# Two graph attention layers on one core: later loads moved into the timetable, two buffers for x2, and new orders of the first and last turns

## The chip, the cores and the metric

The kernel runs on one core of a Trainium2 chip. The time is device microseconds of one execution, the median of several runs. The core's engines are TensorE (PE, matrix products and transposes), VectorE (DVE), ScalarE (ACT), GpSimd (POOL) and SyncE (SP, which here only issues DMA transfers). Each works through its own instructions in their written order; between engines there are only semaphores.

## The reference

128 graphs of 128 nodes with 256 features go through two layers. Shortened:

```python
# layer A: attention, four hops, norm
q, k, v = (x @ W.T + b for W, b in ...)              # 8 heads of 32
p = softmax(where(adj == 0, -16384, q @ k.T))
z = v
for _ in range(4):
    z = 0.9 * (p @ z) + 0.1 * v
x = norm(x + z) * gamma + beta
# layer B: attention with an edge bias, then an MLP
n = norm(x) * ln1_g + ln1_b
p = softmax(q @ k.T / sqrt(32) + where(adj > 0, 0.1 * adj * adj, -inf))   # q, k, v of n
x = x + (p @ v) @ wo + bo
n = norm(x) * ln2_g + ln2_b
out = x + gelu(n @ w1 + b1) @ w2 + b2
```

## The kernel before

The 128 graphs are taken as 64 pairs. All work on a pair is cut into 84 named steps, such as `qA` (the q projection of layer A) or `z0` (the first hop), and the step of pair g is written `qA.g`. One list, the timetable, puts all steps of all pairs in an order. Every engine walks the whole list and does its own part of each step, waiting on semaphores; so the list fixes the order of instructions on each engine and nothing else. There is no other planner.

The middle of the list is made from `ORDER`: in a turn each step is done once, with a lag that says for which pair. The first 9 turns are replaced by the written-out list `HEAD`, the last 8 by `TAIL`, in which pairs are counted from the end (`d1.1` is of the last pair, `d1.2` of the one before it). 52 turns stay between.

The names, with the engine in brackets where it is not PE and an evacuation:
- `lt`, `lx`, `laA`, `laB`, `st` [SP]: load x transposed, x, the adjacency of layer A and of B; store the output. `xs` [POOL] splits x transposed into a high and a low part.
- `qA kA vA`, `qB kB vB`: projections, each of 12 products of 256 columns; q and k are evacuated by ACT, v by DVE. `sA`, `sB`: scores.
- `msA`, `msB` [POOL] masks, `eb` [DVE] the edge term for `msB`. `mA00` to `mA11` [DVE] add the mask and take row maxima, `eA00` to `eA11` [ACT] the exps, `rA0`, `rA1` [DVE] reciprocals, `wA0`, `wA1` [POOL] normalise in two halves each, `pA00` to `pA11` turn the probabilities (evacuated by ACT or DVE). The first digit is the graph of the pair. The same with B.
- `z0` to `z3`: hops, evacuated by ACT; `h0` to `h3`: turned back, evacuated by DVE. `xv` [POOL]: the share of v plus x.
- `y0 i0 n0`, `y1 i1 n1`, `y2 i2 n2`: norms, as statistics [DVE], root [POOL], scaling [DVE]. `g`, `b1`, `b2` [POOL]: gamma and beta, plus bo, plus b2. `tB`, `tC`: turn the normed rows, split by ACT (high) and DVE (low).
- `pv`: probabilities times v, split by ACT and DVE. `o`: output projection; DVE adds it into the tile `x2`. `u0` to `u3`: first MLP product with gelu on ACT (four instructions each), `c0` to `c3` [DVE] its low part; `d0`, `d1`: second MLP product, 24 products each, added into `x2` by DVE and stored.
- Once only: `Wf`, the fold of the norms' biases into the projections' biases, PE with products of one column; `Wq Wk Wv Wo Wu0 Wu1 Wd0` to `Wd3`, the splits of weights into high and low (high on ACT, low on DVE, for `Wd` on POOL).

PE's results go to a ring of 4 PSUM banks in list order (`table.bank`); a step waits until the one four before it is evacuated. The scores have banks of their own.

Ahead of its part of the list SP issues, in this order: Wq of A, x transposed of pair 0, Wk and Wv of A, adjacency A of pair 0, wq wk wv of B, w1 with two columns, x of pair 0, wo, w2 in four parts, three columns, five rows (each spread over 128 partitions). ACT issues four columns and one row of its own. The raw weights lie in tiles that the pairs use later: wq, wk, wv, wo in `probs`, w1 in `probsT_B`, w2 in `x1b`, `nx`, `n2`, `x2`. DVE's `output` (L752) waits until both halves of `x2` of the pair before are stored.

Of the kernel before, what the change touches and what calls it, by code (L numbers as in the profile page):

```python
# [55 lines left out]
wA1.2 n1.0 z2.1 xv.2 b1.0 i0.1 wA0.2 qA.3 laA.1 h2.1 tB.0 g.1 z3.1 pA10.2 pA11.2 h3.1 rA0.2 y0.1 n0.1 mB00.0 kB.0 xs.4
lt.3 mB01.0 qB.0 kA.3 sB.0 mB10.0 pA00.2 pA01.2 mB11.0 eB00.0 y1.1 vA.3 i1.1 eB10.0 rB1.0 lx.1 eB11.0 vB.0 z0.2 n1.1
eB01.0 laA.2 wB1.0 rB0.0 sA.3 kA.4 h0.2 pB10.0 mA00.3 tB.1 pB11.0 z1.2 pB00.0 mA01.3 pB01.0 eA00.3 h1.2 eA01.3 kB.1
mA10.3 rA0.3 mA11.3 wB0.0 xv.3 pv.0 laA.3 eb.1 wA0.3 z2.2 qB.1 h2.2 msB.1 eA10.3 o.0 pA00.3 y2.0 eA11.3 mB00.1 mB01.1
rA1.3 sB.1 i2.0 laB.1 mB10.1 b1.1 n2.0 z3.2 wA1.3 msA.4 mB11.1 eB00.1 qA.4 vA.4 h3.2 eB10.1 tC.0 eB01.1 laA.4 pA01.3  # L60
mA00.4 rB0.1 sA.4 pA10.3 eB11.1 pA11.3 xv.4 mA01.4 wB0.1 u0.0 vB.1 eb.2 y0.2 c0.0 rB1.1 z0.3 u1.0 i0.2 lt.4 pB00.1
h0.3 lx.2 u2.0 n0.2 c1.0 u3.0 wB1.1 c2.0 pB01.1 c3.0 z1.3 pB10.1 pB11.1 y1.2 mA10.4 n1.2 mA11.4 eA00.4 g.2 b2.0 eA10.4
h1.3 lx.3 d0.0 eA01.4 pv.1 rA0.4 d1.0 eA11.4 tB.2 rA1.4 qA.5 o.1 y2.1 i1.2 kB.2 qB.2 pA00.4 z2.3 sB.2 pA10.4 n2.1
eB00.2 mB00.2 xs.5 h2.3 mB01.2 msB.2 mB10.2 mB11.2 kA.5 lt.5 tC.1 msA.5 z3.3 wA0.4 vB.2 eB10.2 lx.4 eB01.2 h3.3 pA01.4
laB.2 y0.3 vA.5 eB11.2 u0.1 b1.2 laA.5 i2.1 rB0.2 u1.1 rB1.2 n0.3 pA11.4 c0.1 wA1.4 eb.3 u2.1 u3.1 c1.1 c2.1 y1.3 c3.1
mA00.5 lx.5 sA.5 z0.4 pB00.2 pB01.2 n1.3 pB10.2 mA01.5 eA00.5 i0.3 eA01.5 wB0.2 mA10.5 st.0 h0.4 lt.6 rA0.5 d0.1 tB.3
g.3 wB1.2 d1.1 eA10.5 laA.6 z1.4 mA11.5 i1.3 pB11.2 kB.3 h1.4 qB.3 z2.4 pv.2 eA11.5 sB.3 eB00.3 mB00.3 h2.4 rA1.5
mB01.3 pA00.5 o.2 y2.2 mB10.3 z3.4 mB11.3 qA.6 n2.2 eB01.3 h3.4 b2.1 y0.4 pA10.5 vA.6 rB0.3 kA.6 tC.2 vB.3 n0.4 eB10.3
pA01.5 eB11.3 msB.3 pA11.5 u0.2 u1.2 wA0.5 xs.6 xv.5 rB1.3 wA1.5 i2.2 b1.3 msA.6 mA00.6 b2.2 laB.3 lt.7 c0.2 sA.6 i0.4
y1.4 c1.2 z0.5 mA01.6 u2.2 wB0.3 u3.2 mA10.6 g.4 n1.4 qA.7 h0.5 pB10.3 eb.4 xs.7 st.1 tB.4 i1.4 wB1.3 c2.2 pB00.3  # L70
msB.4 mA11.6 z1.5 pB01.3 qB.4 laB.4 eA00.6 pB11.3 kB.4 eA01.6 c3.2 pv.3 xv.6 laB.5 h1.5 rA0.6 wA1.6 eA10.6 lx.6 eA11.6
d0.2 d1.2 wA0.6 rA1.6 mB00.4 mB01.4 sB.4 z2.5 mB10.4 o.3 eB00.4 eB01.4 eB10.4 y2.3 h2.5 rB0.4 i2.3 vA.7 wB0.4 kA.7
n2.3 b2.3 pA00.6 pA10.6 z3.5 mB11.4 pA01.6 tC.3 sA.7 eB11.4 pA11.6 h3.5 y0.5 rB1.4 pB00.4 n0.5 u0.3 st.2 z0.6 u1.3
c0.3 mA00.7 u2.3 mA01.7 c1.3 h0.6 u3.3 c2.3 msA.7 y1.5 c3.3 pB10.4 vB.4 eA00.7 mA10.7 laA.7 b1.4 z1.6 n1.5 pB01.4 d0.3
eA01.7 tB.5 eA10.7 pB11.4 mA11.7 eb.5 rA1.7 eA11.7 d1.3 h1.6 i0.5 qB.5 rA0.7 lt.8 kB.5 pv.4 mB00.5 z2.6 sB.5 pA00.7
# [5 lines left out]
laA.4 lt.3 h3.6 xs.4 wA0.5 tC.8 y0.6 eB10.7 z0.5 wA1.5 vA.4 eB11.7 eb.6 vB.7 h0.5 u0.8 sA.4 mA00.4 n0.6 z1.5 pB00.7  # L81
xv.5 c0.8 u1.8 i2.8 lx.5 h1.5 msA.4 u2.8 u3.8 rB1.7 qA.3 z2.5 c1.8 c2.8 b1.7 mA01.4 pB10.7 xs.3 c3.8 y1.6 pB01.7
pB11.7 eA00.4 n1.6 h2.5 laB.5 d0.8 eA01.4 pv.7 mA10.4 rA0.4 wB0.7 z3.5 mA11.4 tB.6 i0.6 d1.8 rA1.4 b2.8 eA10.4 h3.5
y0.5 g.6 eA11.4 wB1.7 o.7 y2.7 qB.6 kB.6 msB.6 pA10.4 pA00.4 pA01.4 pA11.4 eB00.6 mB00.6 sB.6 n2.7 z0.4 n0.5 kA.3
mB01.6 mB10.6 tC.7 eB01.6 i1.6 h0.4 mB11.6 wA0.4 eB10.6 xv.4 vB.6 rB0.6 eb.5 y1.5 vA.3 mA00.3 n1.5 eB11.6 c0.7 lx.4
st.8 c1.7 u0.7 sA.3 z1.4 u1.7 rB1.6 pB00.6 u2.7 wA1.4 h1.4 tB.5 mA01.3 u3.7 mA10.3 z2.4 laA.3 msA.3 pB01.6 pB10.6
pB11.6 eA00.3 qB.5 h2.4 kB.5 c2.7 z3.4 c3.7 mA11.3 mB00.5 eA01.3 rA0.3 eA10.3 pv.6 mB01.5 eA11.3 sB.5 rA1.3 d0.7
eB10.5 mB10.5 i2.7 lx.3 i0.5 d1.7 eB00.5 h3.4 y0.4 pA10.3 mB11.5 o.6 y2.6 vA.2 b1.6 eB01.5 g.5 qA.2 eB11.5 rB0.5 kA.2
n0.4 n2.6 lt.2 pA11.3 pA00.3 vB.5 wB0.6 pA01.3 rB1.5 tC.6 y1.4 mA00.2 mA01.2 sA.2 z0.3 u0.6 n1.4 h0.3 qA.1 u1.6 mA10.2
c0.6 i1.5 laA.2 pB00.5 eb.4 c1.6 tB.4 u2.6 u3.6 xv.3 pB01.5 qB.4 wB1.6 c2.6 b2.7 eA10.2 msB.5 kB.4 eA00.2 xs.2 c3.6  # L90
pB10.5 lt.1 lx.2 pB11.5 mA11.2 mB00.4 eA11.2 d0.6 rA1.2 sB.4 wA0.3 z1.3 mB01.4 pv.5 d1.6 msA.2 eA01.2 h1.3 eB00.4
rA0.2 eB01.4 mB10.4 pA10.2 laB.4 mB11.4 o.5 wA1.3 y2.5 z2.3 pA00.2 st.7 pA11.2 pA01.2 h2.3 i0.4 kA.1 z0.2 n2.5 z3.3
tC.5 h0.2 eB10.4 rB0.4 eB11.4 vB.4 i2.6 h3.3 y0.3 b1.5 mA00.1 g.4 u0.5 xs.1 i1.4 sA.1 z1.2 rB1.4 n0.3 pB00.4 u1.5 c0.5
pB01.4 h1.2 wB0.5 b2.6 laB.3 u2.5 c1.5 pB10.4 mA01.1 u3.5 pB11.4 c2.5 wB1.5 c3.5 z2.2 mA10.1 laA.1 pv.4 eA00.1 y1.3
h2.2 eb.3 st.6 eA01.1 st.5 n1.3 eA10.1 d0.5 msB.4 rA0.1 wA1.2 d1.5 msA.1 wA0.2 mA11.1 tB.3 z3.2 i2.5 o.4 b1.4 eA11.1
y2.4 rA1.1 wB0.4 h3.2 n2.4 qB.3 kB.3 y0.2 i0.3 wB1.4 mB00.3 g.3 mB01.3 pA00.1 sB.3 tC.4 xv.2 n0.2 pA10.1 eB00.3 mB10.3
mB11.3 pA11.1 vA.1 eB01.3 pA01.1 i1.3 eB10.3 eB11.3 b2.5 rB0.3 y1.2 vB.3 rB1.3 u0.4 z0.1 c0.4 n1.2 u1.4 pB00.3 wA0.1
pB01.3 msB.3 u2.4 c1.4 i2.4 wA1.1 h0.1 tB.2 i0.2 u3.4 pB10.3 b1.3 g.2 wB0.3 eb.2 i1.2 pB11.3 c2.4 kB.2 c3.4 qB.2 wB1.3
xv.1 pv.3 z1.1 mB00.2 mB01.2 sB.2 mB10.2 d0.4 mB11.2 lx.1 d1.4 eB00.2 rB0.2 msB.2 h1.1 o.3 eB01.2 y2.3 eB10.2 z2.1
b2.4 eB11.2 h2.1 n2.3 pB00.2 z3.1 rB1.2 pB01.2 h3.1 laB.2 tC.3 y0.1 vB.2 pB10.2 n0.1 u0.3 c0.3 wB0.2 i2.3 u1.3 pB11.2  # L100
# [830 lines left out]
```

## Time and profile before

| what | us |
|---|---|
| runs | 2314.32, 2314.19, 2317.76 |
| median | 2314.32 |
| the profiled execution | 2317.23 |
| its span | 2315.4 |
| PE busy | 2266.6 (98%) |
| ACT busy | 1926.8 (83%) |
| DVE busy | 1749.9 (76%) |
| POOL busy | 1520.4 (66%) |

The span goes from the first to the last instruction of the core; the execution's own time has 1.8 us around it. Busy times count instructions at work. Products are pipelined, so their durations overlap and the distance from start to start is what counts. The granted clock is TensorE's, as a share of 2.4 GHz; half of it is the other level, 1.2 GHz.

### The profile page before, as it was taken

What the parts mean: (1) busy time and instruction counts of PE and PEld (TensorE: products, weight loads), DVE (VectorE), ACT (ScalarE), POOL (GpSimd) and SP (SyncE); (2) the same over time, 40 slices, a digit from 0 to 9 for tenths busy, and PEclk for the clock granted to TensorE, in tenths of its full rate; (3) what the DMA queues carried; (4) which work ended last, traced back from release to release, by engine and by line L of the source; (5) the groups of instructions that cost most, each with busy time, mean ns of one, the idle gap of its engine ahead of it and who ended that gap; (6) DMA issues with size and microseconds to landing.
All of it is one profiled execution on the core that took longest, in us unless ns stands there. A gap on an engine that the chain in (4) does not pass through costs nothing. (4 is left out here: it accounts for less than half of the span.)

```text
span 2315.4 us, 78263 instructions
## 1 busy us (share of the span) xinstructions
PE 2266.6 (98%) x29492; PEld 2154.3 (93%) x29492; DVE 1749.9 (76%) x6993; ACT 1926.8 (83%) x6478; POOL 1520.4 (66%) x1613
## 2 busy tenths in 40 slices
...
DMA packets 95781, 76.88 MB, mean 33 GB/s; under 512 B 9648, under 2 KB 95152, under 8 KB 95408
## 3 DMA queue, kind: packets, MB, share of 16 engines
q1 hardware_dynamic: 94176, 71.73, 10.0%
...
q10 hardware_dynamic: 1232, 0.14, 0.0%
...
## 5 line engine op out<-in xcount | busy, mean ns | idle before, releaser
L580 ACT ACTIVATE probs<-probs,negmax 128x128 f32<-128x128 f32 x2048 | 797.0, 398 | 28.1 <-DVE negmax L704 22.0
L862 POOL TENSOR_TENSOR probs<-probs,rinv 128x512 f32<-128x512 f32 x512 | 534.3, 1064 | 138.7 <-DVE rinv L718 138.4
L580 ACT ACTIVATION_READ_ACCUMULATOR probs<-probs,negmax 128x1 f32 x2048 | 402.3, 196 | 0.0
L601 ACT ACTIVATE zT<-ring_ps 128x512 f32<-128x512 f32 x256 | 157.8, 617 | 182.4 <-PE ring_ps L459 182.2
L377 PE MATMUL ring_ps<-inT_C_high,w_high 128*128 128x256 f32 x1024 | 302.4, 295 | 5.3 <-DVE inT_C_low L675 4.0
L515 PE MATMUL ring_ps<-w_high,hT_high 128*128 128x256 f32 x1024 | 296.8, 290 | 1.0 <-DVE hT_low L790 1.0
L451 PE MATMUL ring_ps<-ident,probs 128*128 128x128 f32 x2048 | 293.3, 276 | 3.1 <-ACT hT_high L621 1.6
L515 PE MATMUL ring_ps<-w_low,hT_high 128*128 128x256 f32 x1024 | 286.5, 280 | 0.0
L515 PE MATMUL ring_ps<-w_high,hT_low 128*128 128x256 f32 x1024 | 286.2, 279 | 0.0
L377 PE MATMUL ring_ps<-inT_C_high,w_low 128*128 128x256 f32 x1024 | 285.8, 279 | 0.0
L377 PE MATMUL ring_ps<-inT_C_low,w_high 128*128 128x256 f32 x1024 | 285.8, 279 | 0.0
L790 DVE TENSOR_TENSOR hT_low<-hidden,hT_high 128x512 fp32r<-128x512 f32 x256 | 231.4, 905 | 62.5 <-ACT hT_high L621 56.2
L451 PEld LDWEIGHTS ring_ps<-ident,probs 128*128 128x128 f32 x2048 | 227.4, 141 | 29.5 <-issue 26.9
L704 DVE CUSTOM_DVE_ANT_0 probs<-score_ps,mask_B 128x128 f32<-128x128 f32 x1024 | 228.4, 283 | 29.2 <-PE score_ps L442 29.2
L868 POOL TENSOR_TENSOR rstd<-moments,eps 128x2 f32<-128x2 f32 x192 | 39.4, 205 | 313.3 <-DVE moments L773 312.9
L704 DVE CUSTOM_DVE_ANT_0 probs<-score_ps,mask_A 128x128 f32<-128x128 f32 x1024 | 229.5, 283 | 4.3 <-PE score_ps L442 3.1
L621 ACT ACTIVATE hidden<-ring_ps,b_col 128x256 f32<-128x256 f32 x512 | 218.8, 490 | 13.9 <-PE ring_ps L377 9.9
L621 ACT ACTIVATE hT_high<-ring_ps,b_col 128x256 fp32r<-128x256 f32 x512 | 220.9, 503 | 0.0
L459 PE MATMUL ring_ps<-probsT_A,z 128*32 128x128 f32 x6144 | 209.2, 277 | 1.2 <-DVE z L738 1.0
L757 DVE TENSOR_TENSOR x<-ring_ps,x1b 128x512 f32<-128x512 f32 x64 | 44.2, 690 | 209.9 <-PE ring_ps L377 203.6
L377 PEld LDWEIGHTS ring_ps<-inT_C_high,w_high 128*128 128x128 f32 x1024 | 194.7, 190 | 7.9 <-DVE inT_C_low L675 4.8
L377 PEld LDWEIGHTS ring_ps<-inT_C_low,w_high 128*128 128x128 f32 x1024 | 195.2, 191 | 0.0
...
## 6 DMA issues: line engine op xcount, KB each, us to landing
xT_sb<-in_xT_dram SPq DMA_DIRECT2D x64, 256.0 KB, 3.1
x_sb<-in_x_dram SPq DMA_DIRECT2D x64, 256.0 KB, 2.8
out_dram<-x SPq DMA_DIRECT2D x128, 128.0 KB, 1.9
...
qT_B<-in_L_gnn_Wq_dram SPq DMA_DIRECT2D x1, 256.0 KB, 3.6
kT_B<-in_L_gnn_Wk_dram SPq DMA_DIRECT2D x1, 256.0 KB, 4.8
```

Source lines behind the costliest of these rows:

```text
L377: mm = pe.matmul(dst, left(a, kc), right(b, kc), start=(n == 0), stop=(n == len(pairs) - 1))
L451: mm = pe.transpose(ring(name, g)[:, r * P:(r + 1) * P], probs[:, UNIT[l, b], half * HR + r, :], ident[:, :])
L459: mm = pe.matmul(ring(name, g)[r * HD:(r + 1) * HD, (b * C + c) * P:(b * C + c + 1) * P], src[:, b, h * HD:(h + 1) * HD], prT[:, b, h, :], ...
L515: mm = pe.matmul(ring(name, g)[:, 0:H], hT[a][:, f, b * P:(b + 1) * P], w2_p[c][:, f, :], start=(n == 0), stop=(n == len(pairs) - 1))
L580: e = act.activation(probs[:, u, h, :], probs[:, u, h, :], ACT.Exp, bias=negmax[:, u, h:h + 1], scale=-1.0, accum_out=sums[:, u, h:h + 1])
L601: act.activation(zT[k][:, :, :, :], ring(name, g).rearrange("p (b c n) -> p b c n", b=GB, c=C), ACT.Copy).then_inc(s_out[name], 1)
L621: e = act.activation(dst[:, i, :], ring(name, g)[:, i * T:(i + 1) * T], ACT.Gelu, bias=b1_col[:, 2 * f + i:2 * f + i + 1])
L704: t = dve.tensor_tensor_reduce(probs[:, u, h, :], score_ps[:, r, (b * C + half) * P:(b * C + half + 1) * P], mask[l][:, b, :], -1.0, HIGHE ...
L757: dve.tensor_tensor(x2[:, :, :], ring(name, g).rearrange("p (b n) -> p b n", b=GB), x1b[:, :, :], ALU.add).then_inc(s_out[name], 1)
L790: dve.tensor_tensor(hT[1][:, 2 * f:2 * f + 2, :], hidden[:, f % 2, :, :], hT[0][:, 2 * f:2 * f + 2, :], ALU.subtract).then_inc(s_h_low, 1)
L862: pool.tensor_tensor(probs[:, u, hs, :], probs[:, u, hs, :], rinv[:, u, hs].unsqueeze(2).to_broadcast([P, HR, P]), ALU.mult).then_inc(s_pr ...
L868: pool.tensor_tensor(rstd[n][:, :, :], moments[n][:, :, 1:2], eps[:, :].unsqueeze(1).to_broadcast([P, GB, 1]), ALU.add).then_inc(s_shifted ...
```

## The change

- SP issues ahead of the list only x transposed of pair 0 and the three weights of layer A. All other loads become steps: `LB` (wq, wk, wv), `Lc` (three columns and the row bvB), `Lu` (w1 and two columns), `Lo` (wo), `Ld` (w2), `Lr` (four rows); the first `laA` and `lx` now issue too. SP's list begins laA.0 LB.0 laB.0 Lc.0 lt.0 Lu.0 laA.1 lx.0 lt.1 laB.1 Lo.0 Ld.0 lt.2 laA.2 lx.1 Lr.0. The semaphore `rest` is parted into `columns` (waited for by `fold`) and `rows` (by `scale_shift`).
- `x2` has two buffers, used by even and odd pairs, each with its semaphore; `output` of pair g waits for the store of pair g - 2. The same index stands in `store`, `spread`, `norm`, `down` and `plus_b2`.
- `HEAD` and `TAIL` are new orders of the same steps. PE's part of the new head begins qA.0 kA.0 vA.0 sA.0 Wf.0 vA.1 qA.1 kA.1 pA10.0 pA11.0 pA00.0 pA01.0 sA.1 z0.0 h0.0 z1.0 kA.2 h1.0 qA.2 z2.0, and ACT's Wk.0 Wq.0 qA.0 kA.0 Wu1.0 eA00.0 eA10.0 eA11.0 eA01.0 Wu0.0 qA.1 Wv.0 kA.1 pA10.0 pA00.0 Wd2.0 z0.0. `ORDER` stays.

Of the two lists, the beginning of the first and the end of the second are shown.

```diff
-eb.0 qA.0 lx.0 laB.0 xs.0 laA.0 kA.0 eA00.0 vA.0 mA00.0 sA.0 msA.0 eA01.0 xs.1 mA01.0 lt.0 qA.1 lt.1 mA10.0 mA11.0
...
+laA.0 xs.0 Wk.0 Wq.0 LB.0 eb.0 laB.0 mA00.0 qA.0 mA01.0 msA.0 mA10.0 kA.0 Lc.0 Wu1.0 mA11.0 eA00.0 vA.0 lt.0 xs.1 sA.0
+Wf.0 rA1.0 msB.0 eA10.0 wA1.0 vA.1 wA0.0 Lu.0 eA11.0 rA0.0 msA.1 eA01.0 Wu0.0 qA.1 Wv.0 kA.1 pA10.0 pA11.0 pA00.0
+laA.1 xv.0 pA01.0 sA.1 Wd2.0 eb.1 xs.2 mA00.1 z0.0 mA01.1 eA00.1 eA01.1 mA10.1 h0.0 xv.1 eA10.1 mA11.1 wA0.1 rA0.1
+wA1.1 z1.0 msA.2 Wd1.0 eA11.1 kA.2 h1.0 qA.2 z2.0 lx.0 rA1.1 pA00.1 Wd0.0 Wd3.0 h2.0 pA01.1 pA10.1 pA11.1 mA00.2 z3.0
...
-u1.2 u2.2 c0.2 c1.2 c2.2 c3.2 u3.2 i2.2 pB10.1 pB00.1 b2.2 pB11.1 b1.1 pB01.1 wB0.1 d0.2 pv.1 d1.2 o.1 y2.1 wB1.1 n2.1
-tC.1 i2.1 c0.1 u0.1 u1.1 c1.1 u2.1 u3.1 c2.1 c3.1 d0.1 d1.1 st.1 b2.1
+u0.3 wB1.2 pB10.2 qB.1 rB0.2 kB.1 wB0.2 pB00.2 pB01.2 c0.3 msB.1 u1.3 i2.2 wB0.1 pB11.2 u2.3 c1.3 b1.1 pv.2 u3.3 c2.3
+mB00.1 sB.1 c3.3 eB00.1 o.2 eB01.1 y2.2 mB01.1 st.2 mB10.1 n2.2 eB10.1 d0.3 rB0.1 mB11.1 d1.3 tC.2 vB.1 eB11.1 rB1.1
+pB00.1 pB01.1 c0.2 u0.2 pB10.1 u1.2 pB11.1 u2.2 c1.2 pv.1 c2.2 c3.2 u3.2 o.1 y2.1 n2.1 d0.2 tC.1 d1.2 c0.1 u0.1 c1.1
+u1.1 u2.1 wB1.1 u3.1 c2.1 c3.1 i2.1 d0.1 b2.2 b2.1 st.1 d1.1
...
+SET_UP = {"LB": ("load_proj",), "Lu": ("load_up",), "Lo": ("load_wo",), "Ld": ("load_down",), "Lc": ("load_columns",),
+          "Lr": ("load_rows",), "Wf": ("fold",), "Wo": ("split_o",)}
...
-        x2 = sb("x2", [P, GB, H])
+        x2 = [sb(f"x2_{i}", [P, GB, H]) for i in range(2)]
...
-        w2_raw = [x1b, nx, n2, x2]
+        w2_raw = [x1b, nx, n2, x2[0]]
...
-            weight(rawA["q"][:, :, :], WqT, "Aq")
             sp.dma_start(xT_sb[:, :, :], xT_v[0]).then_inc(s_xT, 16)
-            weight(rawA["k"][:, :, :], WkT, "Ak")
-            weight(rawA["v"][:, :, :], WvT, "Av")
-            sp.dma_start(adj_sb["A"][:, :, :], adj_v[0]).then_inc(s_adj["A"], 16)
...
+            for n, w in (("q", WqT), ("k", WkT), ("v", WvT)):
+                weight(rawA[n][:, :, :], w, "A" + n)
+
+            def load_proj(name, g):
+                for n, w in (("q", wq), ("k", wk), ("v", wv)):
+                    weight(rawB[n], w, "B")
+
+            def load_up(name, g):
+                weight(w1_raw, w1, "up")
+                column(h2_col, ln2_b, "up")
+                column(g2_col, ln2_g, "up")
+
+            def load_wo(name, g):
+                weight(rawB["o"], wo, "o")
+
+            def load_down(name, g):
+                for f, t in enumerate(w2_raw):
+                    sp.dma_start(t[:, :, :], w2.rearrange("(c p) n -> p c n", p=P)[:, 2 * f:2 * f + 2, :])\
+                        .then_inc(s_in["down"], 16)
+
+            def load_columns(name, g):
+                for t, w in ((colB["q"], lbq), (colB["k"], lbk), (b1_col, b1)):
+                    column(t, w, "columns")
+                row(bvB_row, lbv, "columns")
+
+            def load_rows(name, g):
+                for t, w in ((gamma_row, gamma), (beta_row, beta), (bo_row, bo), (b2_row, b2)):
+                    row(t, w, "rows")
...
-                if g or l == "B":
-                    sp.dma_start(adj_sb[l][:, :, :], adj_v[g]).then_inc(s_adj[l], 16)
+                sp.dma_start(adj_sb[l][:, :, :], adj_v[g]).then_inc(s_adj[l], 16)
...
-                    sp.dma_start(out_v[g][:, b, :], x2[:, b, :]).then_inc(s_stored, 16)
+                    sp.dma_start(out_v[g][:, b, :], x2[g % 2][:, b, :]).then_inc(s_stored[g % 2], 16)
...
-                if g:
-                    dve.wait_ge(s_stored, 16 * GB * g)
-                dve.tensor_tensor(x2[:, :, :], ring(name, g).rearrange("p (b n) -> p b n", b=GB), x1b[:, :, :],
+                if g >= 2:
+                    dve.wait_ge(s_stored[g % 2], 16 * GB * (g // 2))
+                dve.tensor_tensor(x2[g % 2][:, :, :], ring(name, g).rearrange("p (b n) -> p b n", b=GB), x1b[:, :, :],
```

## Rows read from the trace of the kernel before

**Rows 1.** Windows: length, busy us of each engine, granted clock, DMA share, GB/s.
```profile
16.00:28.00 12.00, 0.17 (x1) 0.17 (x2) 2.93 (x21) 1.03 (x5) 2.11 (x3) 0.68 0.49 126
28.00:60.00 32.00, 27.58 (x369) 23.78 (x370) 18.39 (x75) 24.82 (x89) 23.54 (x22) 0.85 0.14 43
60.00:76.00 16.00, 16.00 (x118) 14.69 (x119) 12.22 (x47) 9.51 (x37) 11.21 (x13) 0.68 0.15 43
76.00:320.00 244.00, 240.66 (x3208) 225.55 (x3207) 195.10 (x762) 204.83 (x695) 164.81 (x174) 1.00 0.10 31
320.00:1980.00 1660.00, 1660.00 (x21869) 1585.89 (x21867) 1276.00 (x5197) 1427.85 (x4814) 1124.17 (x1190) 1.00 0.10 32
1980.00:2264.00 284.00, 277.45 (x3569) 261.98 (x3571) 221.51 (x825) 230.56 (x766) 180.84 (x191) 1.00 0.09 28
2264.00:2291.00 27.00, 21.06 (x204) 19.75 (x204) 14.26 (x54) 16.61 (x54) 7.47 (x8) 0.87 0.02 6
2291.00:2316.00 25.00, 15.46 (x102) 14.54 (x100) 6.73 (x14) 6.72 (x17) 2.16 (x3) 0.80 0.05 17
```

**Rows 2.** Timeline of SP's queue, 4 to 29 us: start, us, line, transfer.
```profile
4.49 0.77 SPq L308 DMA_DIRECT2D probs<-in_L_gnn_wv_dram  x1
...
14.97 2.67 SPq L314 DMA_DIRECT2D bvB_row<-in_L_gnn_bv_dram  x1
...
19.58 0.43 SPq L344 DMA_DIRECT2D adj_B<-in_adj_dram  x1
20.05 8.11 SPq L338 DMA_DIRECT2D xT_sb<-in_xT_dram  x2
```

**Rows 3.** Timeline of all engines, first 43 us; in brackets the idle time before.
```profile
13.12 0.84 ACT L572 ACTIVATE kT_A<-ring_ps,colA_k 128x256 f32<-128x256 f32 x2 [1.72 <-PE ring_ps L377]
...
25.07 0.42 DVE L670 SCALAR_TENSOR_TENSOR edges<-adj_B 128x256 f32<-128x256 int32 x1 [15.69 <-DMA adj_B<-in_adj_dram]
...
27.83 0.58 PE L377 MATMUL ring_ps<-inT_A_high,wA_q_high 128*128 128x256 f32 x1 [11.97 <-POOL inT_A_low L843]
...
42.15 1.08 PE L459 MATMUL ring_ps<-probsT_A,v_A 128*32 128x128 f32 x32
```

**Rows 4.** Sources L388 and L391, the fold: ns min/median/max, first and last start.
```profile
L388 PE MATMUL ring_ps<-h_col,probsT_B x32: 250/352/353, 63.5 to 69.0; 128*128 128x1 f32 x32
...
L388 PE MATMUL ring_ps<-h_col,probs x16: 169/250/251, 61.8 to 63.4; 128*128 128x1 f32 x16
...
L391 PE MATMUL ring_ps<-probs,h_col x4: 634/634/774, 69.2 to 70.6; 128*128 128x256 f32 x4
```

**Rows 5.** Timeline, the last 53 us.
```profile
2263.85 1.17 PE L442 MATMUL score_ps<-kT_B,qT_B 32*128 32x128 f32 x32
...
2286.62 0.39 PE L515 MATMUL ring_ps<-w_high,hT_high 128*128 128x256 f32 x1
...
2289.56 0.28 PE L377 MATMUL ring_ps<-wo_high,oT_high 128*128 128x256 f32 x1
...
2292.03 0.69 DVE L757 TENSOR_TENSOR x<-ring_ps,x1b 128x512 f32<-128x512 f32 x1 [1.85 <-DMA out_dram<-x]
...
2295.66 1.12 PE L402 MATMUL ring_ps<-ident,n 128*128 128x128 f32 x4 [4.54 <-DVE n L784]
```

**Rows 6.** DMA issues before 330 us: count, KB, us from issue to landing.
```profile
probs<-in_L_gnn_wv_dram SPq DMA_DIRECT2D x1, 256.0 KB, 7.0
...
g_col<-in_L_gnn_ln_g_dram SPq DMA_DIRECT2D x1, 1.0 KB, 7.8
```

**Rows 7.** Lines: busy us, mean ns of one (page; 0 to 110 us by form).
```profile
L580 ACT ACTIVATE probs<-probs,negmax 128x128 f32<-128x128 f32 x2048 | 797.0, 398 | 28.1 <-DVE negmax L704 22.0
L862 POOL TENSOR_TENSOR probs<-probs,rinv 128x512 f32<-128x512 f32 x512 | 534.3, 1064 | 138.7 <-DVE rinv L718 138.4
...
L535 ACT ACTIVATE wB_q_high<-probs,g_col 128x256 fp32r<-128x256 f32 x2 | 0.9, 498 | 0.0
```

**Rows 8.** Windows again, a stretch inside the head.
```profile
34.00:44.00 10.00, 8.61 (x113) 7.28 (x112) 5.46 (x36) 9.81 (x42) 6.91 (x8) 1.00 0.22 67
```

More of the change, by code:

```diff
@@ L56 @@
[L56 to L75, printed above, removed]
@@ new lines @@
+sA.2 h3.0 i0.0 y0.0 mA01.2 z0.1 h0.1 n0.0 g.0 vA.2 z1.1 h1.1 lt.1 Wo.0 eA00.2 eA01.2 xs.3 mA10.2 y1.0 laB.1 mA11.2
+i1.0 z2.1 b1.0 rA0.2 h2.1 n1.0 Lo.0 eA10.2 vA.3 wA0.2 Ld.0 eA11.2 wA1.2 rA1.2 z3.1 tB.0 qA.3 h3.1 qB.0 kB.0 i0.1 y0.1
+pA00.2 g.1 n0.1 pA10.2 eB00.0 pA11.2 mB00.0 msA.3 mB01.0 i1.1 wB0.0 sB.0 mB10.0 wB1.0 pA01.2 y1.1 mB11.0 lt.2 rB0.0
+kA.3 eB01.0 msB.1 xv.2 wA0.3 vB.0 laA.2 z0.2 sA.3 n1.1 h0.2 msA.4 xs.4 mA00.3 eB10.0 wA1.3 rB1.0 eB11.0 tB.1 lx.1
+mA01.3 pB00.0 z1.2 pB01.0 eA00.3 kB.1 pB10.0 pB11.0 i2.0 eA01.3 h1.2 mA10.3 rA0.3 qB.1 mA11.3 i0.2 pv.0 z2.2 mB00.1
```

105 lines of the change are left out of this document (52 added, 53 removed).

## Prediction

> **What bounds the kernel now.** I read the windows first, to see where TensorE (PE) stands still. From 320 to 1980 us it is busy 1660 of 1660 us at the full clock [rows 1]: 52 of the 64 pairs run without a gap, and the diff changes neither an instruction of theirs nor their order. Nothing can be won there. All that the change can give or take is at the two ends, so I count what TensorE loses in them.
>
> Head, from 16 us on: idle 11.83 (16 to 28), 4.42 (28 to 60), 0 (60 to 76) and 3.34 us (76 to 320), together 19.6 [rows 1]. The mean clock of 0.85 over 32 us and 0.68 over 16 us [rows 1] is a mixture of full and half speed (2.4 and 1.2 GHz): 2 x 0.15 x 32 = 9.6 us and 2 x 0.32 x 16 = 10.2 us at half speed, nearly all with PE busy, so 4.8 + 5.1 = 9.9 us lost. Head: 29.5 us.
> Tail: idle 6.55, 5.94 and 25.00 - 15.46 - 0.6 (the span ends at 2315.4) = 8.94, together 21.4 us. The half-speed time is 7.0 and 10 us [rows 1]; PE works in about 3.8 and 6.8 of these (it stands still in the rest), so 5.3 us lost. Tail: 26.7 us.
>
> Then the timeline of SP, of the head and of the tail, for the causes.
> - The first gap has one cause, the in-order queue of SP. The transposed x of pair 1 is issued at 20.05 us, behind 26 other issues, and adjacency B at 19.58 [rows 2]. VectorE's first step of the table is eb.0: it waits 15.69 us for adjacency B and holds the evacuation of vA.0 and all maxima; PE restarts at 27.83, after 11.97 us [rows 3].
> - The fold of biases (Wf.0) holds PE with products of one column: 32 of them take 352 ns each, from 63.5 to 69.0, and four wide ones 634 ns [rows 4]. With the first sixteen it is 9.4 us, and the granted clock falls to 0.5 in it.
> - At the end: o.1 may not overwrite x2 before the store of pair 62 has left (VectorE stands 1.85 us), then a whole norm lies bare between o.1 and tC.1 (PE idle 4.54 us), then PE comes back at half speed [rows 5].
>
> **The change, part by part.**
> *Loads.* The table's steps take the second loads behind adjacency B and the one wide row. Nothing is dropped: it is a matter of place in SP's queue. The third B weight keeps its issue at about 4.5 us and lands 7.0 later, at 11.5 [rows 2, 6]. Adjacency B goes out at about 5.3 instead of 19.58. Pair 1's x now has 18 issues ahead and must wait behind laA.1, which waits for the first mask; at some 0.5 us an issue it leaves at 11 to 14 and lands by 15 to 19 (7.0 us for a weight, 7.8 for the last column, [rows 6]), instead of some 2 us before PE's 27.83.
> *A rule beside this row.* The Trainium skill, "DMA: Bandwidth & Descriptors", section "Anatomy of one DMA", gives about 2 us fixed plus bytes at 436 GB/s. The landings of [rows 6] are three times that, since the transfers queue behind each other. By the page pair 1's x would be there some 4 us sooner; the fold in front of it would hide that, so the sum would be the same within 1 us.
> *New head order.* ACT now takes Wk.0 and Wq.0 first, four instructions of 0.50 us [rows 7], 0.9 a pair as they overlap, so 11.5 + 1.8 = 13.3, then qA.0 and kA.0 at 0.84 each [rows 3]: 15.0. sA.0 starts at 15.0 instead of about 14.7: +0.3. It ends at 16.2. Next on PE is the fold, moved forward from 61.8. It needs w1 and two columns that now stand behind adjacency B, three columns and a row whose issue alone took 2.67 us [rows 2]; the last column is issued at 9.2 to 12.1 and lands 7.8 later [rows 6]: 17.0 to 19.9. I take 17.5. The fold is 6.1 us if the full clock holds (its first 16 products start 107 ns apart, 61.8 to 63.4; 48 x 0.107 + half of the last 2.0, [rows 4]) and 9.4 as seen; I take 8.5, to 26.0, since PE did little before it. Then vA.1 and qA.1 (12 products each, 1.42 us at full, 2.56 at half speed; the 24 of d1.2 took 2.94 [rows 5]) to 30.7, kA.1 to 32.1, four turns of probabilities 2.2, sA.1 1.2, z0.0 1.0: 36.5 us. The other engines are there in time: the sixteen exps, 0.398 us each [rows 7], start behind the first maxima at 17 and, with Wu steps between, end at 24, and two steps of normalise at 2 x 1.06 us each [rows 7] end near 31.7, just before the turns at 32.1.
> Before, z0.0 ended at 43.2 [rows 3] with qA.2 and kA.2 (2.8 us) already done and the fold (6.1 us of full-speed work) not. Lead = 43.2 - 36.5 + 6.1 - 2.8 = 10.0 us; between 7.5 (late column) and 12.5 (early one).
> Behind this point the kernel before still loses 6.5 us of idle time (3.1 to 60 us, 3.34 after it) and about 6.8 us to the clock, of which 3.3 are the fold's own (9.4 - 6.1), already paid in the 36.5. The new order has the same chains of hops and the same setup work on ACT and VectorE, and VectorE is 80% busy from 76 to 320 [rows 1], so I leave the rest as it was: +3.3 from the fold, with 4 either way. Head: 13.3 us won, 6 to 19.
> *w2 and Wo.* They are now issued behind laB.1, which waits for the second layer's mask, itself behind the split of pair 1: about 20 us, landed near 29.5 with 7 to 8 us. ACT wants w2 at Wd2.0, ahead of the evacuation of z0.0, at about 32. Nothing, with 2.5 us in hand; if the cover is gone every us late is a us on PE. The four rows go out with Lr.0 near 33 and are wanted by g.0 near 48: nothing.
> *Two x2 buffers.* In the steady part VectorE's wait before x2 is for PE, not for the store, so nothing there. At the end it takes off 0.8 us (o.1 is through at 2289.56 + 1.4 + 0.2 = 2291.2, the evacuation starts at 2292.03 [rows 5]). Its weight is that o.1 may stand ahead of d0.2 and d1.2: with one buffer that order could not run at all. The second buffer adds no instruction, and the stores wait for the same things.
> *New tail order.* After sB.1 (start 2263.85, [rows 5]) the old order took 51.5 us for 31.7 us of full-speed work (vB, o and eight u at 1.42 each, 14.2; four d, 11.4; four turns, two tC, pv and sB.1, 6.1); the loss, 19.8, is most of the tail's. The new one keeps o.2, d0.3 and d1.3 (7.2 us) behind sB.1, so 38.9 us of work covers the same chain of maxima, exps (16 x 0.40), reciprocals and normalise (4 x 1.06, [rows 7]). pB00.1 is ready about 7 us after sB.1, and PE reaches it after 9.1. Then pv.1, u3.2, o.1, d0.2, tC.1, d1.2, u0.1: the last norm, 3.6 us from VectorE's 2292.03 to tC.1's 2295.66 [rows 5], lies beside d0.2 (2.9), about 0.8 bare; d1.2 hides the 1.4 us of splitting tC.1; PE never stops long, so the clock should stay. Left: 0.8 + 0.4 (o.1 on oT) + 0.5 (last low part) + 2.9 (last evacuation and store, as now) + 1 to 3 of small waits, about 6.5. Before sB.1 the old order lost 6.6; I take the same, 4 to 11, for chains there that the new order shifts too. So 13 to 14 instead of 26.7: 12.5 won, 6 to 18.
> **Sum.** 13.3 + 12.5 = 25.8 us. The profiled execution took 2317.2 (span 2315.4): 2291.4, span 2289.6. The median of the runs, 2314.3, lies 2.9 below it, so 2288.5; I say 2289.
>
> **The rivals.**
> *The clock does not come back in the head (chance 0.10).* The fold now stands where PE has done little; if half speed lasts through the thin stretch to z3.0, some 11 us of full-speed work costs 11 us more: about 2300. For: the clock fell in the fold before. Against: from 34 to 44 us PE was busy only 8.61 of 10 us, with turns among its work, and the clock stood at 1.00 [rows 8]. The Trainium skill, "TensorE: Matmul & The Clock Gate", section "Part 4: PE-mode transpose", says that transposes do not count as PE being busy, and the new stretch is full of them. In the stretch from 320 us, with 56 transposes in each pair by the code, the clock is 1.00 [rows 1], so the trace gives that rule little.
> *The lead in the head is eaten by ACT or VectorE (0.08).* PE arrives 10 us early at work that needs the same exps and setup splits; then only the tail counts: about 2302. For: ACT is 84% busy from 76 to 320. Against: it idles nearly all of 16 to 28 [rows 1], which the new order uses.
> *The tail wins nothing, its waits move ahead of sB.1 (0.10):* about 2301. Against: the bare norm is plainly covered.
> *Slower (0.04).* w2 behind laB.1: ACT stands at Wd2.0 ahead of z0.0, and the ramp behind it. It decides only if w2 lands 26 us later than it is wanted, near 58 us: about 2317. SP's order makes that hard to see.
> *The change does as good as nothing (0.04):* both ends find other waits, 2312 to 2316.
> **How the numbers follow.** The forecast, both ends shorter, has 0.64. Its own range: 25.8 with about 9 to either side, 2279 to 2298. To leave out no more than 2 in 10 the range goes over the cases at 2300 to 2302: 2279 to 2304. The limit of 0.2% is 4.6 us, about what a measurement of this kernel can tell from no change. Faster: 0.64 + 0.10 + 0.08 + 0.10 = 0.92; same 0.04; slower 0.04.
>
> **What would show it.** Right: the adjacency B wait gone; PE's first long gap under 3 us; the fold between 16 and 27 us, z0.0 ending near 36; the middle without a gap; tC of the last pair with under 1.5 us of idle ahead, no half-speed stretch after the last o. Wrong: a clock at 0.5 from 27 to 45 us, ACT idle on w2, new waits of PE between 1980 and the last sB, or PE waiting for normalise around 30 to 60 us.

## The result and the profile after

The changed kernel takes 2286.97 us (median of 4 runs, 2285.81 to 2287.87), the kernel before 2315.19 beside it (4 runs): ratio 0.9877, 95% interval 0.9861 to 0.9893, or 28.2 us less. Predicted were 2289 in 2279 to 2304. The profiled execution took 2287.87 us, with a span of 2286.0, 29.4 less than the span before.

Windows of the kernel after, at the head as in [rows 1] and at the end shifted by about 30 us:

```profile
16.00:28.00 12.00, 8.95 (x45) 8.96 (x43) 5.35 (x34) 8.35 (x34) 4.45 (x4) 0.57 0.37 112
28.00:60.00 32.00, 28.44 (x379) 25.08 (x383) 17.56 (x78) 16.85 (x55) 23.68 (x22) 0.89 0.29 88
60.00:76.00 16.00, 12.94 (x159) 11.73 (x152) 10.60 (x37) 11.50 (x44) 12.06 (x13) 0.89 0.10 26
76.00:320.00 244.00, 241.16 (x3231) 228.13 (x3230) 193.16 (x793) 210.81 (x727) 172.54 (x180) 1.00 0.10 31
320.00:1950.00 1630.00, 1630.00 (x21518) 1557.00 (x21517) 1249.40 (x5083) 1398.11 (x4709) 1105.03 (x1167) 1.00 0.11 32
1950.00:2234.00 284.00, 280.80 (x3657) 265.95 (x3656) 228.15 (x886) 241.77 (x810) 190.43 (x203) 1.00 0.09 27
2234.00:2261.00 27.00, 26.89 (x296) 25.69 (x294) 16.13 (x59) 23.66 (x71) 8.73 (x10) 1.00 0.03 11
2261.00:2286.00 25.00, 19.55 (x161) 18.78 (x160) 9.92 (x19) 8.12 (x21) 3.41 (x4) 1.00 0.07 23
```

PE's idle time in the first window has shrunk from 11.83 to 3.05 us, but the clock's mean of 0.57 in that window says that PE works at half speed there. The middle is full as before. The end has no half speed and 5.4 us of idle in its last 25, against 8.9 before, and 0.1 in the 27 us ahead of it against 5.9.

Where the 29.4 us were won is read best from one event of the untouched middle. SP's issue of the same transfer, in the timeline of the kernel before:

```profile
1918.37 0.50 SPq L338 DMA_DIRECT2D xT_sb<-in_xT_dram  x1
```

and of the kernel after:

```profile
1908.48 0.50 SPq L352 DMA_DIRECT2D xT_sb<-in_xT_dram  x1
```

So the head is 1918.37 - 1908.48 = 9.9 us shorter, and the tail 29.4 - 9.9 = 19.5. The same shift stands at 1001.61 against 1011.49. Forecast were 13.3 and 12.5. That the sum came close is luck: one part fell 3.4 us short, the other was 7.0 us better. The shift itself differs between profiles of one kernel: in a repetition of the changed kernel (e0 below) the same transfer stands at 1000.62, 1.0 us earlier.

The head in detail. SP's queue after:

```profile
5.62 0.58 SPq L357 DMA_DIRECT2D adj_B<-in_adj_dram  x1
...
8.06 2.90 SPq L317 DMA_DIRECT2D bvB_row<-in_L_gnn_bv_dram  x1
11.00 0.43 SPq L311 DMA_DIRECT2D probsT_B<-in_L_gnn_w_dram  x1
...
14.14 0.82 SPq L352 DMA_DIRECT2D xT_sb<-in_xT_dram  x1
```

Adjacency B goes out at 5.62, pair 1's x at 14.14 instead of 20.05 [rows 2]. The timeline of PE shows what PE does meanwhile:

```profile
14.85 1.17 PE L457 MATMUL score_ps<-kT_A,qT_A 32*128 32x128 f32 x32 [1.57 <-ACT kT_A L587]
19.07 3.55 PE L403 MATMUL ring_ps<-h_col,probs 128*128 128x1 f32 x16 [3.05 <-DMA g_col<-in_L_gnn_ln_g_dram]
22.48 6.96 PE L403 MATMUL ring_ps<-h_col,probsT_B 128*128 128x1 f32 x32
29.30 2.05 PE L406 MATMUL ring_ps<-probs,h_col 128*128 128x256 f32 x4
30.80 0.78 PE L392 MATMUL ring_ps<-wA_v_high,inT_A_high 128*128 128x256 f32 x1
...
40.18 1.08 PE L474 MATMUL ring_ps<-probsT_A,v_A 128*32 128x128 f32 x32
```

The fold waits 3.05 us for its last column, then all of it runs at half speed: 11.7 us from 19.07 to 30.80, where [rows 4] gave 9.4. z0.0 ends at 41.3.

The end in detail, the timeline of VectorE and POOL in the kernel after, then of PE:

```profile
2263.35 0.68 DVE L772 TENSOR_TENSOR x<-ring_ps,x1b 128x512 f32<-128x512 f32 x1
2264.07 0.75 DVE L784 BATCH_NORM_STATS2 stats<-x 128x6 f32<-128x256 f32 x2
2264.85 0.25 DVE L788 BATCH_NORM_AGGREGATE moments<-stats 128x2 f32<-128x6 f32 x2
...
2266.12 1.26 POOL L910 TENSOR_TENSOR x<-x,b_row 128x512 f32<-128x512 f32 x1
2266.19 1.66 DVE L799 TENSOR_SCALAR n<-x,moments,rstd 128x256 f32<-128x256 f32 x2 [1.09 <-POOL rstd L886]
```

```profile
2241.97 1.17 PE L457 MATMUL score_ps<-kT_B,qT_B 32*128 32x128 f32 x32
...
2267.91 0.66 PE L417 MATMUL ring_ps<-ident,n 128*128 128x128 f32 x4 [2.06 <-DVE n L799]
```

The store's wait ahead of the last o is gone, and PE stands 2.06 us ahead of the last tC instead of 4.54 [rows 5]. From sB.1 to the end it is 44.0 us, for 38.9 of full-speed work.

### The profile page after: what moved, and what is told of

Its sections match the earlier page's. It is cut to its first block, busy times and chain, and to the rows that moved or that the text cites. A ratio compares the mean times of both kernels' runs of the same rounds, so it can differ in the third digit from the quotient of the medians.

```text
span 2286.0 us, 78265 instructions
## 1 busy us (share of the span) xinstructions
PE 2256.0 (99%) x29492; PEld 2148.3 (94%) x29492; DVE 1734.4 (76%) x6993; ACT 1925.5 (84%) x6478; POOL 1524.2 (67%) x1613
## 4 chain that ended last, share of the span: by engine, by line
PE 94%; DVE 2%; ACT 2%; issue 1%; SPq 0%; DMA 0%; POOL 0%; ACTq 0%; DVEq 0%; POOLq 0%
PE ring_ps L392 41%; PE ring_ps L530 15%; PE ring_ps L474 13%; PE ring_ps L466 10%; PE score_ps L457 6%; PE ring_ps L494 5%; PE ring_ps L417 3%; ACT probs L595 1%; DVE probs L719 0%; PE ring_ps L403 0%; DVE hT_low L805 0%; DMA g_col<-in_L_gnn_ln_g_dram 0%; DVE nx L799 0%; ACT hT_high L636 0%; DVE stats L784 0%
## 5 line engine op out<-in xcount | busy, mean ns | idle before, releaser
L805 DVE TENSOR_TENSOR hT_low<-hidden,hT_high 128x512 fp32r<-128x512 f32 x256 | 222.5, 870 | 59.1 <-ACT hT_high L636 52.9
L719 DVE CUSTOM_DVE_ANT_0 probs<-score_ps,mask_B 128x128 f32<-128x128 f32 x1024 | 228.4, 283 | 28.2 <-PE score_ps L457 28.2
L530 PEld LDWEIGHTS ring_ps<-w_high,hT_high 128*128 128x128 f32 x1024 | 192.4, 188 | 2.3 <-DVE probsT_B L744 1.1
```

The costliest lines, as they stand in the source:

```text
L530: mm = pe.matmul(ring(name, g)[:, 0:H], hT[a][:, f, b * P:(b + 1) * P], w2_p[c][:, f, :], start=(n == 0), stop=(n == len(pairs) - 1))
L719: t = dve.tensor_tensor_reduce(probs[:, u, h, :], score_ps[:, r, (b * C + half) * P:(b * C + half + 1) * P], mask[l][:, b, :], -1.0, HIGHE ...
L805: dve.tensor_tensor(hT[1][:, 2 * f:2 * f + 2, :], hidden[:, f % 2, :, :], hT[0][:, 2 * f:2 * f + 2, :], ALU.subtract).then_inc(s_h_low, 1)
```

## The experiments

All ratios are to the kernel before, run on the same chip beside each. There are three groups: e1 to e4 on one chip, e0, e5, e7 and e8 on a second, e6, e9, e11 and e12 on a third. The changed kernel was measured again only on the second (e0). The last four are compared with it through the kernel before, whose medians on the two chips are 2316.2 and 2316.8 to 2317.5. The interval of most ratios reaches 3 to 4 us to either side, so small differences between kernels of two groups are not told apart by the times.

**The ends taken apart.** Four kernels, each with a part of the change.

*e1: two x2 buffers alone.*
```diff
-        x2 = sb("x2", [P, GB, H])
+        x2 = [sb(f"x2_{i}", [P, GB, H]) for i in range(2)]
...
-                if g:
-                    dve.wait_ge(s_stored, 16 * GB * g)
+                if g >= 2:
+                    dve.wait_ge(s_stored[g % 2], 16 * GB * (g // 2))
```


> The kernel before with two x2 buffers alone; loads, head and tail orders as before. My theory: only VectorE's waits for a store in the last turns go (1.85 us bare at the last o), so 0 to 0.8 us less than before, 2314.3 to 2315.2, and a profile in which PE still stands some 4 us ahead of the last tC. Rival, the buffers themselves bring the tail's gain: 10 us or more less.

Ratio 0.9987 (0.9978 to 0.9996), 3.0 us less (0.9 to 5.1). Its last tC:

```profile
2292.81 1.11 PE L404 MATMUL ring_ps<-ident,n 128*128 128x128 f32 x4 [3.68 <-DVE n L786]
```

The idle time ahead of tC fell by 0.86 us (4.54 to 3.68), as forecast. The span of this profile is 3.7 us shorter than before. Besides the 0.86 us, the middle stood 1.2 us earlier in it although nothing ahead of it was changed, and from tC's start to the end it took 18.9 us instead of 19.7: the products behind it came to full speed 5.7 us after tC's start, and 8.0 before. That the shorter wait also shortened the half speed is argued and not shown, and the low end of the interval is the 0.9 us of the wait alone.

*e2: the kernel before with two x2 buffers and the new TAIL.*
```diff
+ e1's edit
- TAIL of the kernel before
+ TAIL of the changed kernel
```


> The kernel before with two x2 buffers and the new TAIL; loads and head as before. Theory, the ends are independent and the whole tail difference of the two profiles is the order's: the middle stays where it was in the kernel before and the end comes 19.5 us earlier, about 2295.7. Rival, the tail's gain needs the new head (engines arriving less backlogged): under 12 us won, above 2303.

Ratio 0.9915 (0.99 to 0.993), 19.7 us less. Its middle stands where it stood (1011.49 for the same transfer as in the kernel before) and its span is 2296.0, so the tail is 19.4 us shorter. The tail's gain needs nothing of the head. The 3.0 us that the buffers gave in e1 are part of it.

*e3: the changed kernel with the old TAIL.*
```diff
- TAIL of the changed kernel
+ TAIL of the kernel before
```


> The changed kernel with the old TAIL; new loads, two x2 buffers, new HEAD. Theory: 9.9 us won at the head (the shift of the middle between the two profiles), plus at most 0.8 of the buffers: 2304.5 to 2305.3. Rival, the head's lead is given back in the tail: 2310 or more.

Ratio 0.9947 (0.9932 to 0.9962), 12.3 us less, of which e1's 3.0 belong to the buffers: 9.3 for the head. In its profile the middle stands 11.0 us earlier (1000.46), 1.1 more than in the kernel after with the same head. The two ends add up: 19.7 + 12.3 - 3.0 = 29.0, against 28.2 for the whole.

*e4: the new loads, the old head order on the other engines.*
```diff
+ SP's part of HEAD: laA.0 LB.0 laB.0 Lc.0 lt.0 Lu.0 lx.0 lt.1 Lo.0 Ld.0 Lr.0, then as before
  all other engines' parts of HEAD and TAIL: as before
```


> The changed kernel with the old TAIL and, in the head, the old order on all engines but SP; SP issues the B weights, adjacency B, the columns and the row, w1, x of pair 0 and x transposed of pair 1 first, then wo, w2 and the rows, then its old list. Theory: PE's first gap ends 4 to 6 us earlier and most of that stays, so 4 us or so of the head's 9.9: about 2311. Rival A, the loads are all of the head's gain: 2305. Rival B, the loads alone do nothing, since the ramp behind them is bound by ACT and VectorE: 2314 to 2315.

Ratio 0.996 (0.9946 to 0.9974), 9.3 us less, 6.3 without e1's 3.0. In its profile the middle's transfer stands at 1005.21, 6.3 us earlier than before. PE restarts 5.7 us earlier than in the kernel before, still behind the split of pair 1's x:

```profile
22.12 0.58 PE L392 MATMUL ring_ps<-inT_A_high,wA_q_high 128*128 128x256 f32 x1 [7.74 <-POOL inT_A_low L858]
```

So the loads alone are some two thirds of the head's gain, more than my 4; the new orders bring the rest. Both rivals fall.

**The fold.** It was the largest miss of the head. Six kernels and the changed kernel itself again.


> The changed kernel as it is, as the base for the other runs on this chip: ratio to the kernel before 0.987 to 0.989, as in its first measurement; the middle of the profile 9 to 11 us earlier than before.

Ratio 0.9878 (0.9862 to 0.9894), median 2287.27. The fold in its profile:

```profile
19.11 2.88 PE L403 MATMUL ring_ps<-h_col,probs 128*128 128x1 f32 x16 [3.12 <-DMA g_col<-in_L_gnn_ln_g_dram]
30.17 0.78 PE L392 MATMUL ring_ps<-wA_v_high,inT_A_high 128*128 128x256 f32 x1
```

The gap is the same, 3.12 us, but the fold takes 11.1 us and not 11.7, since its first products still ran at full speed. z0.0 starts at 39.56.

*e5: the fold behind kA.1.*
```diff
- Wf.0 between sA.0 and vA.1
+ Wf.0 between kA.1 and pA10.0
```


> The changed kernel with Wf.0 moved behind kA.1 in the list (vA.1, qA.1, kA.1 first). Theory, the early fold costs since PE does its 11.8 us at half speed while the split of pair 1 has been ready since 23.3: here PE would start vA.1 at 23.3 instead of 30.8, the fold follows with a faster clock (about 8 us), z0.0 ends 2 to 4 us earlier, and the time falls by 2 to 4 us against the changed kernel. Rival, the fold fills a hole that stays empty here (16 to 23.3), so it is as long or 2 to 5 us longer: in the hole nothing else can run, and half speed returns after it.

Ratio 0.9892 (0.9875 to 0.991), median 2289.66: 2.4 us longer than e0, and no run is faster than e0's slowest (2287.82 to 2292.24 against 2286.74 to 2287.64). The rival holds: PE idles 7.12 us until vA.1 starts at 23.03. The fold itself was faster there (7.5 us from 29.15 to 36.69), which did not pay for the hole: z0.0 starts 2.0 us later than in e0.

*e6: the fold where it was before, behind h1.1.*
```diff
- Wf.0 between sA.0 and vA.1
+ Wf.0 behind h1.1
```


> The changed kernel with Wf.0 back behind h1.1 of pair 1, where the kernel before had it. Theory, the early fold is worth only what it fills of the hole from 16 to 23.3 us: here vA.1 starts at 23.3, the fold comes at about 60 us at mostly full speed and covers the hop chains' gaps of 3 us from 60 to 76, so within 2 us of the changed kernel. Rival, moving the fold forward is where the new head's gain comes from: 5 us or more longer.

Ratio 0.9878 (0.9863 to 0.9893), median 2288.48: the same as the changed kernel within the noise. z0.0 starts at 33.09 instead of 40.18, and the fold gives it back later, in the 8.6 us from 54.64 to 63.28. No gain or loss by its place can be told here.

*e7: the three columns and the wide row behind pair 1's x.*
```diff
- SP's part of HEAD: laA.0 LB.0 laB.0 Lc.0 lt.0 Lu.0 laA.1 lx.0 lt.1 laB.1
+ SP's part of HEAD: laA.0 LB.0 laB.0 lt.0 Lu.0 laA.1 lx.0 lt.1 Lc.0 laB.1
```


> The changed kernel with Lc.0 (three columns and the wide row bvB, whose issue holds SP 2.9 us) moved behind lt.1 in SP's list, so w1 and its columns and x of pair 0 and 1 are issued about 4.8 us earlier. Theory, PE's wait ahead of the fold (3.05 us, until the last column of w1 has landed) is that issue's price: the wait falls under 1 us and the time by 2 to 3 us against the changed kernel. Rival, the transfers share the same engines and land no sooner, or the later row holds the fold's evacuation on VectorE: no change, or 1 to 2 us longer.

Ratio 0.9857 (0.9842 to 0.9873), median 2282.39 (2281.03 to 2283.9) against e0's 2287.27 (2286.74 to 2287.64): 4.9 us less, the lowest median of all kernels here, and 33 us below the kernel before by the ratio. SP's queue and PE's timeline:

```profile
6.31 0.58 SPq L311 DMA_DIRECT2D probsT_B<-in_L_gnn_w_dram  x1
...
11.37 0.47 SPq L352 DMA_DIRECT2D xT_sb<-in_xT_dram  x1
...
14.04 1.32 SPq L317 DMA_DIRECT2D bvB_row<-in_L_gnn_bv_dram  x1
```

```profile
14.62 1.17 PE L457 MATMUL score_ps<-kT_A,qT_A 32*128 32x128 f32 x32 [1.40 <-ACT kT_A L587]
15.72 1.95 PE L403 MATMUL ring_ps<-h_col,probs 128*128 128x1 f32 x16
17.53 6.78 PE L403 MATMUL ring_ps<-h_col,probsT_B 128*128 128x1 f32 x32
```

The wait ahead of the fold is gone, and the fold's first sixteen products run at full speed. Against e0 the fold starts 3.4 us earlier and is 1.1 us shorter (10.0 against 11.1), and z0.0 starts 4.8 us earlier. The gain is larger than the 2 to 3 us I expected by that 1.1 and because no other wait took the start's 3.4 back. Three columns and the row were moved together, and their shares were not parted.

*e8: 28 extra products ahead of the fold's wait.*
```diff
             def fold(name, g):
+                take(name, g)
+                for i in range(28):
+                    pe.matmul(ring(name, g)[:, H:2 * H], wA["k"][0][:, 0, 0:P], wA["v"][0][:, 0, :], start=True, stop=True)
                 pe.wait_ge(s_in["B"], 16 * 5)
                 pe.wait_ge(s_in["up"], 16 * 3)
-                take(name, g)
```


> The changed kernel with 28 extra products of 256 columns (their result is overwritten, they leave out nothing) between sA.0 and the fold's wait, so PE is busy through its 3 us gap. Theory A, the clock fell to half at 17.7 us because of the gap: with it filled the first sixteen of the fold run at full speed (1.7 instead of 3.5 us) and the rest in part; 2 to 4 us less than the changed kernel. Theory B, the fold's one-column products themselves let the clock fall, gap or not, as in the kernel before at 64.7 us: at most 1 to 2 us less, and the part on w1 still at about 180 to 215 ns apart instead of 107.

Ratio 0.9862 (0.9847 to 0.9878), median 2283.39: 3.9 us less than e0, by work that has no use but to keep PE busy. The fold's products by source, first of the kernel after, then of e0, then of e8:

```profile
L403 PE MATMUL ring_ps<-h_col,probsT_B x32: 352/352/352, 22.5 to 29.1; 128*128 128x1 f32 x32
L403 PE MATMUL ring_ps<-h_col,probs x16: 344/352/353, 19.1 to 22.3; 128*128 128x1 f32 x16
```

```profile
L403 PE MATMUL ring_ps<-h_col,probsT_B x32: 352/352/352, 21.8 to 28.5; 128*128 128x1 f32 x32
L403 PE MATMUL ring_ps<-h_col,probs x16: 242/352/353, 19.1 to 21.6; 128*128 128x1 f32 x16
```

```profile
L404 PE MATMUL ring_ps<-h_col,probsT_B x32: 250/352/352, 21.1 to 26.3; 128*128 128x1 f32 x32
L404 PE MATMUL ring_ps<-h_col,probs x16: 164/250/250, 19.4 to 20.9; 128*128 128x1 f32 x16
```

Theory A holds for the first sixteen (250 ns instead of 352) and part of the rest; theory B for most of the rest, whose median is still 352. That the gap let the clock fall ahead of the fold is so in the profile of the kernel after, but not in e0's. From the mean clock of the windows 16 to 19 and 19 to 23 us (0.80 and 0.50; in e0 1.00 and 0.60; in e8 1.00 and 0.95) I estimate that it fell at 17.8 us in the kernel after, in the gap, at 19.8 in e0, inside the fold, and at 22.6 in e8. So the products ahead of the fold kept it up some 3 us longer. Against e0 the fold is 2.4 us shorter (8.6), z0.0 starts 2.9 us earlier and the middle stands 3.8 earlier; the last us comes behind z0.0, where the clock's mean from 60 to 76 us is 1.00 instead of 0.89.

*e9: both edits.*
```diff
+ e7's order of the loads
+ e8's 28 products
```


> Both edits together on the changed kernel: the three columns and the row behind lt.1 (run e7), and the 28 extra products ahead of the fold (run e8). Theory A, they save different things (the wait of 3 us; the half speed of the fold): 7 to 8 us less than the changed kernel, ratio to before near 0.984 to 0.985. Theory B, they fill the same hole: with the fold's input there at 15.7 us the extra products only delay it, so no better than e7 alone (0.9857), or up to 3 us worse.

Ratio 0.9862 (0.9846 to 0.9879), median 2285.56: nothing beyond either alone. With the fold's inputs there early, the extra products only push its start from 15.72 to 20.03. Theory B.

*e12: pair 1's x right behind adjacency B, the fold late.*
```diff
- SP's part of HEAD: laA.0 LB.0 laB.0 Lc.0 lt.0 Lu.0 laA.1 lx.0 lt.1 laB.1
+ SP's part of HEAD: laA.0 LB.0 laB.0 lt.0 lt.1 Lu.0 laA.1 lx.0 Lc.0 laB.1
+ Wf.0 behind h1.1
```


> The changed kernel with the fold back behind h1.1 (run e6) and x transposed of pair 1 issued right behind adjacency B, then w1 and its columns, adjacency A of pair 1, x of pair 0, and the three columns and the row last. It asks whether the hole from 16 to 23.3 us is one of landing. Theory A, it is: pair 1's x lands by 13, vA.1 follows sA.0 at once, the clock stays full, z0.0 ends near 29 instead of e6's 34; 3 to 6 us less than the changed kernel and level with e7 (ratio 0.9855 to 0.987). Theory B, the chain of maxima, exps and normalise to the first turns bounds the ramp whatever PE does: vA.1 is early, but the turns start no earlier than in e6 (29.8 us) and the time stays at 0.9878 within 1 us.

Ratio 0.9869 (0.9852 to 0.9887), which holds what both theories say; the profile lies between them. Pair 1's x leaves at 6.41 us:

```profile
6.41 0.40 SPq L352 DMA_DIRECT2D xT_sb<-in_xT_dram  x1
```

vA.1 follows the scores with no gap now, and the turns start at 24.17 instead of 29.82, but behind a wait for normalise:

```profile
24.17 3.12 PE L466 MATMUL ring_ps<-ident,probs 128*128 128x128 f32 x12 [3.38 <-POOL probs L877]
28.14 0.66 PE L466 MATMUL ring_ps<-ident,probs 128*128 128x128 f32 x4 [0.85 <-POOL probs L877]
```

z0.0 starts at 30.46, 2.6 us earlier than in e6, and the middle stands 1.1 us earlier (1000.74 against 1001.80). So the hole was one of landing, and near 24 us the chain of exps and normalise becomes the bound.

**The tail.** *e11: the last norm laid bare again.*
```diff
- u3.2 o.1 y2.1 n2.1 d0.2 tC.1 d1.2 c0.1 u0.1
+ u3.2 d0.2 d1.2 o.1 y2.1 n2.1 tC.1 c0.1 u0.1
```
(on POOL, `i2.1` goes behind `b2.2`)

> The changed kernel with the end of the TAIL put back in one point: d0.2 and d1.2 ahead of o.1, its norm and tC.1, so the last norm lies bare again (i2.1 behind b2.2 on POOL, which this needs). Theory, the bare norm and the half speed after it are the second half of the tail's gain: PE idles about 4 us ahead of tC.1 and some 7 us of work after it run at 1.2 GHz, so 5 to 8 us more than the changed kernel. Rival, the tail's gain is made ahead of it (sB.1's chain): under 3 us more.

Ratio 0.9894 (0.9879 to 0.9909), median 2292.05: 3.7 us more than e0 by the ratios, 4.8 by the medians. In the profiles the tail, from the middle's transfer to the end, is 6.3 us longer than in the kernel after, but the profiled execution was the slowest of the four. PE waits 3.68 us ahead of tC.1 and the clock's mean is 0.57 in the twelve us around it:

```profile
2270.00:2282.00 12.00, 8.00 (x39) 7.61 (x40) 2.79 (x8) 3.53 (x9) 2.16 (x3) 0.57 0.00 1
```

So the covered norm is worth some 4 to 6 of the tail's 19.5 us, between the theory and its rival. The larger part is made ahead of it: in the two windows ahead of the last 25 us the idle time fell from 6.55 + 5.94 to 3.20 + 0.11 us, and 7 us of half speed are gone. Which of the moved steps does it was not tried.

## Why the prediction was right, and where its terms were off

The direction, the size of the whole (28.2 us against the 25 to 26 forecast) and the two places were right; the middle did not move, its period is 34.88 us in both kernels. Point by point:

- *The cause of the first gap: shown.* VectorE's 15.69 us wait for adjacency B is gone, pair 1's x leaves 5.9 us earlier, and the loads alone are 6.3 us (e4). In e12, where x leaves at 6.41, PE's wait for it is gone. What adjacency B alone is worth was not tried.
- *The start of the fold: right within its bounds* (17.0 to 19.9, measured 19.07; I took 17.5, 1.6 early). The row's issue stood in the way as I had priced it (2.90 us, 2.67 in [rows 2]), and e7 shows that moving it with the three columns was worth 4.9 us.
- *The fold's length: the term that was mis-sized.* I took 8.5 us, between 6.1 and the 9.4 of [rows 4]. It was 11.7, and 11.1 in e0. The 9.4 was itself a mixture, its first sixteen products had run at 250 ns; at half speed throughout each takes 352. My upper bound was thus no bound: a row at mixed clock had been taken as the slow case. With the late start this put z0.0's end at 41.3 instead of 36.5, and the lead there at 43.2 - 41.3 + 6.1 - 2.8 = 5.2 us, below the 7.5 that I gave as its low end. e8 shows that this is the clock's price: with PE kept busy ahead of it the fold is 2.4 us shorter than in e0, and 3.9 us come back in all.
- *Behind z0.0 the head won 9.9 - 5.2 = 4.7 us*, where I had 3.3 for the fold's own half speed. From z0.0 to 320 us the half speed cost about 6.8 us before and 1.8 after (the clock's mean of 0.89 from 60 to 76 us), while PE's idle time grew from 7.1 to 9.4: 2.8 us net. I had left everything there but the fold as it was, and it did not stay so; 2 us stay open. With the fold late (e6) the lead at z0.0 is 43.2 - 34.2 - 2.8 = 6.2, and 3.5 are won behind it.
- *The rival of the clock in the head* came half true. The half speed lasted from before the fold to about 35 us, but not through the stretch to z3.0, where the clock was 1.00 with PE busy 15.55 of 19 us (41 to 60). Beside it I had set what the Trainium skill says ("TensorE: Matmul & The Clock Gate", Part 4: transposes do not count as PE being busy), and had called the stretch full of them. It is not: 36 of its some 250 products are transposes. So this trace says little about that rule, for or against it.
- *The landings.* The fit of the Trainium skill that I had set beside [rows 6] ("DMA: Bandwidth & Descriptors", "Anatomy of one DMA") is given there for transfers that GpSimd issues; these are issued by SP. Pair 1's x landed 6.3 us after its issue.
- *ACT and w2:* w2 landed at 27.70 + 5.0 = 32.7 us, some 6 us before ACT came to it (39.0); no wait shows. I had 29.5 and 32: laB.1, behind which w2 stands, left at 25.25 instead of about 20, and this did no harm because ACT came 7 us later too.
- *Two buffers:* the 0.8 us was right for the wait (0.86 in e1); the kernel gained 3.0 (0.9 to 5.1), 2 of which I had not foreseen and cannot assign with certainty.
- *The tail: right in kind, 7 us short.* From sB.1 to the end I had 38.9 + 6.5 = 45.4, measured 44.0. The norm ahead of tC.1 was bare for 2.06 us, not 0.8: its scaling took 1.66 us instead of the 0.73 of before, with POOL's plus_b2 beside it (see the last section). What I had left at zero was the stretch before sB.1: its idle time fell from 6.6 to 3.3 us. With 1.4 for sB.1's part that makes 4.7 more than forecast. Another 1.1 is my own sum: 6.5 + 6.6 left of 26.7 are 13.6 won, and I wrote 12.5. The last 1.5 lies between the accounting by losses (26.7 to 8.7, 18.0) and the shift (19.5), and stays open.

Of the signs named for a right prediction four were missed: PE's first gap was 3.05 us and not under 3, the fold ran to 30.8 and not 27, z0.0 ended at 41.3 and not near 36, tC's wait was above 1.5. The wait of adjacency B gone, the middle without a gap and no half speed after the last o were seen. Of the signs of a wrong one only the clock at 0.5 behind 27 us showed, and it lasted to 35 and not to 45.
